# A vision transformer layer on one core: small products behind the gate projection, a softplus behind the next decay, and a reordered start

## The reference

```python
h = layernorm(tokens @ W) * gamma
x = layernorm(h)                                # 16 heads of 64, 256 tokens
q, k = silu(x @ Wq), silu(x @ Wk); v = x @ Wv
log_alpha = -softplus(x @ Wa + ba)              # one per token and head
cum = cumsum(log_alpha, over tokens)
attn = (q @ k.T) * exp(cum_i - cum_j)           # for j <= i, else 0
o = attn @ v                                    # per head
o = (o - mean) / sqrt(var + eps) * gn_w + gn_b  # mean, var over tokens and one head
h = h + (o * sigmoid(x @ Wg)) @ Wo
# the top 2 of 8 experts per token, softmax weights, gelu
h = h + sum_e w_e * (gelu(layernorm(h) @ w1[e] + b1[e]) @ w2[e] + b2[e])
```

## Time and profile before

| | us |
|---|---|
| median of 3 runs | 1318.67 |
| lowest, highest | 1316.14, 1321.25 |
| the profiled execution | 1316.64 |
| its span | 1314.6 |
| PE busy | 1251.5 (95%) |
| PEld busy | 1072.4 (82%) |
| DVE busy | 824.6 (63%) |
| ACT busy | 858.2 (65%) |
| POOL busy | 425.4 (32%) |

### The profile page before, as it was taken

How to read it: one execution, slowest core, us unless ns; L and a number is a source line. 1 busy time by engine, 2 the same in 40 slices (tenths; PEclk the granted TensorE clock), 3 DMA queues, 4 the chain that set the end, 5 groups by cost and what they waited for, 6 DMA issues and landing times. The chain is left out here.

```text
span 1314.6 us, 27299 instructions
## 1 busy us (share of the span) xinstructions
PE 1251.5 (95%) x8534; PEld 1072.4 (82%) x8534; DVE 824.6 (63%) x2120; ACT 858.2 (65%) x2019; POOL 425.4 (32%) x524
## 2 busy tenths in 40 slices
PE   6799999999999999999999999999999999999996
PEld 4576877877877877878878768889899999989996
DVE  4456466566666566665665566657788888555562
ACT  3567567667567567576576465637788888666662
POOL 2111211241241241241241132154445544434433
PEclk8899999999999999999999899999999999999998
DMA  5423222242231341341331335468987886888883
GB/s 185 143 100 90 78 91 88 77 129 74 93 122 55 110 132 49 116 131 47 114 116 56 101 95 193 151 186 245 278 232 220 230 242 184 250 271 269 251 239 83
DMA packets 125607, 194.46 MB, mean 148 GB/s; under 512 B 16272, under 2 KB 91504, under 8 KB 125360
## 3 DMA queue, kind: packets, MB, share of 16 engines
q1 hardware_dynamic: 110864, 175.37, 41.5%
q0 software_dynamic: 13584, 17.26, 6.4%
q10 hardware_dynamic: 1056, 0.55, 0.2%
HBM read 167.40 MB, written 29.05 MB: 149 GB/s over the span
## 5 line engine op out<-in xcount | busy, mean ns | idle before, releaser
L1190 PE MATMUL bank<-xn_sp,big_r 128*128 128x512 f32 x1152 | 315.2, 411 | 2.2 <-DVE big_r L1694 1.7
L1190 PEld LDWEIGHTS bank<-xn_sp,big_r 128*128 128x128 f32 x1152 | 206.6, 190 | 56.4 <-issue 2.4
L837 ACT ACTIVATE dec_x<-dec_x,ncum 128x256 f32<-128x256 f32 (+1 forms) x512 | 189.7, 444 | 10.4 <-POOL dec_x L663 10.4
L1717 DVE TENSOR_TENSOR att<-bank,dec_x 128x384 f32<-128x384 f32 x256 | 130.6, 552 | 102.7 <-PE bank L1229 100.8
L663 POOL TENSOR_SCALAR_AFFINE_SELECT dec_x<-dec_x 128x256 f32<-128x256 f32 x256 | 101.7, 427 | 225.2 <-DMA dec_x<-cum_scratch 224.9
L1535 PE MATMUL bank<-big_r 128*128 128x256 f32 x1296 | 168.0, 286 | 1.9 <-ACT mid_f L907 1.3
L1535 PEld LDWEIGHTS bank<-big_r 128*128 128x128 f32 x1296 | 160.5, 192 | 3.6 <-ACT mid_f L907 1.7
L714 POOL TENSOR_SCALAR mid_f<-mid_f,dec_x 128x256 f32<-128x256 f32 x71 | 77.5, 1096 | 184.7 <-DVE mid_f L1968 182.3
L720 POOL DMA_INDIRECT out<-mid_f,tok x71 | 117.8, 1660 | 53.7 <-POOL mid_f L714 20.2
L1984 DVE TENSOR_TENSOR big_r<-mid_f,big_r 128x256 fp32r<-128x256 f32 x216 | 91.2, 423 | 69.5 <-ACT big_r L927 69.5
L907 ACT ACTIVATE mid_f<-bank,h 128x256 f32<-128x256 f32 x216 | 101.3, 478 | 43.9 <-PE bank L1535 21.6
(11 more groups left out here) (231 smaller groups left out, 2224.5 us busy)
## 6 DMA issues: line engine op xcount, KB each, us to landing
big_f<-in_L_ffn_w SPq DMA_DIRECT2D x68, 1024.0 KB, 6.4
dec_x<-cum_scratch SPq DMA_DIRECT2D x128, 384.0 KB, 3.5
big_w<-in_L_ffn_w SPq DMA_DIRECT2D x12, 1024.0 KB, 6.4
mid_f<-expert_rows SPq DMA_DIRECT2D x27, 261.0 KB, 3.2
h<-h_scratch SPq DMA_DIRECT2D x8, 512.0 KB, 4.6
out<-h SPq DMA_DIRECT2D x16, 256.0 KB, 4.0
xt<-in_x SPq DMA_DIRECT2D x15, 256.0 KB, 3.8
h_scratch<-h SPq DMA_DIRECT2D x15, 256.0 KB, 2.6
```

The lines of the kernel that those rows point to most:

```text
L837: act.activation(d, d, ACT.Exp, bias=ncum[p % 2][:, NS * u + s, 2 * c + hh:2 * c + hh + 1]).then_inc(M["exp_done"], 1)
L1190: mm = pe.matmul(bank[target][:, :], wp[:, k, c * P:(c + 1) * P], xp[:, k, :], start=(k == 0 and j == 0), stop=(k == EC - 1 and j == 2))
L1717: dve.tensor_tensor(att[hh][:, :], bank[4 + hh][:, 0:LW], dec[n % RING][:, hh, :], ALU.mult).then_inc(M["mult_done"], 1)
```

## The change

- **Order within a step, PE.** `gn_var` (steps 0 and 5), `turn(2p+2)` (step 1) and `logits(p+1)` (step 4) move from between `keys` and `gates` to behind `gates`, ahead of the second weighted sum; `logits` goes behind `out_proj`.
- **ACT.** In `last_step`, `keep_o(p, 6)` comes first instead of behind `xn_hi` and the first `y_hi`. `softplus(p+1)` in step 5 moves from ahead of `tanh_k` to behind the second `decay`. `keep_xnT` and `scaled_h` of step 1 move behind `tanh_g`.
- **DVE.** `decay_logits` moves from the end of step 4 to the head of step 5; in step 0 `embed` comes ahead of `affine`, in step 5 `log_decay` ahead of `affine`.
- **The start.** SP waits for the token weights, the four constants and image 1 before it issues the first weight loads. ACT splits weight 3 ahead of softplus, and `scaled_h(0)`, `scaled_h(1)` go behind `tanh_g(0, 0)`; both decays come last. PE runs `cum(0)` ahead of the values and `cum_rows(0)` behind the first. DVE moves `weight_lo(2)` behind `silu_q`.
- **Tiles.** Image 1's h and normalised tokens lie in `h2` and `xn2` instead of in the buffer of the values, so `keep_v` no longer waits for the stores of h.

```diff
         eps0 = sb("eps0", [P, NS])
         pick = sb("pick", [P, TP, TOPK, X])
+        h2 = sb("h2", [P, TP, E])
+        xn2 = sb("xn2", [P, TP, EW])
...
-        side_h = [h1, mid_f[:, 2816:3328].rearrange("p (s n) -> p s n", s=NS)]
-        side_n = [xn1, mid_f[:, 3328:3840].rearrange("p (s n) -> p s n", s=NS)]
+        side_h = [h1, h2[:, 0:NS, :]]
+        side_n = [xn1, xn2[:, 0:NS, 0:E]]
...
             load_patches(0)
             load_patches(1)
+            sp.wait_ge(M["wt_in"], 32)
+            sp.wait_ge(M["c_in"], 64)
+            sp.wait_ge(M["xt_in1"], 32)
             load_weight(0)
             load_weight(1)
             load_patches(2)
...
                 if p == 0 and t >= NS and n == 0:
                     act.wait_ge(M["tok_ps"], 2)
-                    act.wait_ge(M["h_out"], 32)
...
             def last_step(p):
                 main, nxt = pair(p), pair(p + 1)
+                if main:
+                    keep_o(p, 6)
                 if nxt:
                     xn_hi(p + 1)
                 if main:
                     y_hi(p, 0, 0)
-                    keep_o(p, 6)
...
-                if c == 5 and nxt:
-                    softplus(p + 1)
                 if c == 6 and main:
                     affined(p, 0, 0)
                 if main:
@@ -982,12 +983,11 @@
                     decay(p, c + 1, 1)
                     if c in (1, 2):
                         keep_v(p, c + 4, 0)
+                if c == 5 and nxt:
+                    softplus(p + 1)
...
-                if c == 1 and nxt:
-                    keep_xnT(2 * p + 2)
-                    scaled_h(2 * p + 2)
...
                 if main:
                     tanh_g(p, c + 1)
+                if c == 1 and nxt:
+                    keep_xnT(2 * p + 2)
+                    scaled_h(2 * p + 2)
...
             xn_hi(0)
+            weight_hi(3)
             softplus(0)
+            tanh_q(0, 0)
+            keep_v(0, 0, 2)
+            keep_cum(0)
+            for i in range(1, TP):
+                keep_v(0, i, 2 + i)
+            tanh_k(0, 0)
+            tanh_g(0, 0)
             scaled_h(0)
             scaled_h(1)
-            tanh_q(0, 0)
-            keep_cum(0)
-            weight_hi(3)
-            for i in range(TP):
-                keep_v(0, i, 2 + i)
             decay(0, 0, 0)
-            tanh_k(0, 0)
-            tanh_g(0, 0)
             decay(0, 0, 1)
...
-                if c == 0 and post:
-                    gn_var(p - 1, 1)
-                if c == 1 and nxt:
-                    turn(2 * p + 2)
...
-                if c == 4 and nxt:
-                    logits(p + 1)
-                if c == 5 and main:
-                    gn_var(p, 0)
...
                 if main:
                     gates(p, c + 1)
+                if c == 0 and post:
+                    gn_var(p - 1, 1)
+                if c == 5 and main:
+                    gn_var(p, 0)
+                if c == 1 and nxt:
+                    turn(2 * p + 2)
                 if c == 3 and nxt:
                     turn(2 * p + 3)
                 if c == 4 and post:
                     out_proj(p - 1, 1, 1, 7, "h2_done", 2 * p - 1)
+                if c == 4 and nxt:
+                    logits(p + 1)
...
             queries(0, 0)
+            cum(0)
             values(0, 0, 2, "s1_xnT", 2)
+            cum_rows(0)
             values(0, 1, 3, "s1_xnT", 2)
-            cum(0)
             values(0, 2, 4, "s1_xnT", 2)
-            cum_rows(0)
...
+                if c == 5 and nxt:
+                    decay_logits(p + 1)
                 if c == 5 and post:
                     residual(2 * p - 1)
...
                 if c == 0:
+                    if nxt:
+                        embed(2 * p + 2)
                     if post:
                         affine(2 * p - 1)
-                    if nxt:
-                        embed(2 * p + 2)
...
-                if c == 4 and nxt:
-                    decay_logits(p + 1)
                 if c == 5:
+                    if nxt:
+                        log_decay(p + 1)
                     if main:
                         affine(2 * p)
-                    if nxt:
-                        log_decay(p + 1)
...
-            weight_lo(2)
             running_sums(0)
             silu_q(0, 0)
+            weight_lo(2)
             weight_lo(3)
```

More of the change, by code:

```diff
@@ L166, in vit_layer @@
         xs = sb("xs", [P, EC, SP2])
-        h2 = sb("h2", [P, TP, E])
-        xn2 = sb("xn2", [P, TP, EW])
         cumT = sb("cumT", [TP * H, P])
```

## The result

The changed kernel takes 1332.91 us (median of 4 runs, 1331.56 to 1336.52); the kernel before, beside it, 1319.58 (1316.14 to 1321.25). The ratio is 1.0109, with an interval of 1.008 to 1.0138: about 14 us slower. The profiled execution took 1332.95 us with a span of 1330.9, so 16.3 more span than before. I had forecast 1324.0. The time is 9 us above that. It lies in my whole range (1311 to 1334), but not in the forecast's own (1317 to 1331); the whole range went that high for a late gate at the start (rival C), which did not come, so it is luck that it holds the time.

A forecast was written before the change was run, and what follows sets the result against it. TensorE was taken as the bound; -7.5 + 8.95 + 2.0 + 1.0 + 0.9 = +5.35 on 1316.64 gave 1322.0, plus 2.03 to the median 1324.0 us. Forecast's own range 1317 to 1331, whole range 1311 to 1334.

The forecast's parts named there:

- rival C: Start: wa_sb still lands near 14 us, so the weights start 6 us later; +6 us, 1330, chance 0.11.
- step 7, copy first: Step 7: keep_o(p,6) first on ScalarE shortens PE's waits and keeps its clock up; -7.5 us, bounds -6 to -9.
- softplus late, pairs 1 to 6, full clock: Step 6: scores wait goes, but route and decayed(6,0) come later; +1.0 us net in each of pairs 1 to 6.
- the clock behind it: Step 6, pairs 1 to 6: no clock fall behind the new 1.4 us gap counted in the sum.
- log_decay ahead of affine, pair 0: Step 6 of pair 0: +0.95 us delay, plus 2.0 for low clock after about 2.45 us of PE idle.
- embed ahead of affine: Steps 0 and 1: pair 1's weighted sum ends about 1.2 us later, later pairs 0.15 each; +2.0, bounds +1 to +5.
- small products: Turn, logits and variance products beside the second weighted sum may lose overlap; +1.0 us, bounds 0 to 3.
- start: Start: first weighted sum at 51.5 after about 11 us of PE idle, then low clock; +0.9 us, bounds -1 to +3.5.
- rival B: Step 6 of every pair: clock falls behind the new gap, six times 2.0 us more; 1336, chance 0.10.
- the second chain: Step 6: log_decay waits for Ln ahead of affine, delaying GpSimd's rsqrt and decayed(6,0) from 312.83 to 313.86.
- A: Step 6: softplus has room, the old waits vanish with nothing in return; -4.2 instead of +8.95, 1310.8, chance 0.16.
- D: Softplus on ScalarE: table loads hold it longer than their rows, 2.76 us in six pairs; +16.6, 1340.6, chance 0.02.

The follow-up runs named there:

- e3: The kernel before with keep_o(p, 6) first in last_step on ScalarE and nothing else; 1310.98 us, ratio 0.9932.
- e13: The kernel before with softplus(p+1) in step 5 moved behind the second decay and nothing else; 1336.03 us, ratio 1.0143.
- e6: The changed kernel with affine ahead of log_decay again in step 5 on VectorE; 1331.47 us, ratio 1.0091.
- e7: The changed kernel with affine ahead of embed again in step 0; 1330.00 us, ratio 1.0081.
- e4: The kernel before with only gn_var, turn and logits behind gates and decay_logits at the head of step 5; 1318.35 us, ratio 1.0009.
- e8: The kernel before with the change's whole new start alone, including the tiles of image 1; 1318.98 us, ratio 1.0001.
- e5: The changed kernel with keep_x2(2p-2) ahead of keep_o(p,5) in step 6 on ScalarE; 1328.83 us, ratio 1.0076.
- e2: The changed kernel with store_cum(0) and the four decay loads ahead of the two h stores on SP; 1325.17 us, ratio 1.0045.
- e11: The changed kernel with softplus behind tanh_k but ahead of decay(6,1), and keep_x2 ahead of keep_o in step 6; 1311.39 us, ratio 0.9961.
- e1: The changed kernel with softplus(p+1) back ahead of tanh_k in step 5; 1315.79 us, ratio 0.9974.
- e12: The changed kernel with softplus back ahead of tanh_k, store_cum(0) and decay loads before the h stores, embed behind affine; 1299.09 us, ratio 0.9862.
- e14: The changed kernel with softplus ahead of decay(6,1), keep_x2 before keep_o, store_cum(0) and decay loads before h stores, embed behind affine; 1298.31 us, ratio 0.9838.

## Why the prediction was right in part, and where it failed

| term | predicted | measured, and by what |
|---|---|---|
| step 7, copy first | -7.5 | -9.0 (e3, 0.0068 x 1318; interval -11.7 to -6.2); -7.1 in its trace |
| softplus late, pairs 1 to 6, full clock | +6.0 (1.0 each) | 1.23 each (e13, pair 1) |
| the clock behind it | 0 | +1.5 or 3.1 in 4 to 6 pairs of 6 |
| softplus late in all | +6.0 | +18.8 (e13, 0.0143 x 1318; 14.5 to 23.1) |
| log_decay ahead of affine, pair 0 | +2.95 | +3.16 (trace of e6) |
| embed ahead of affine | +2.0 | 1.42 in the stretch of pair 0, 0.37 in each later one (trace of e7) |
| small products | +1.0 | pairs 0.32 shorter each; in all +1.2 (e4, -1.3 to +3.6) |
| start | +0.9 | +0.1 (e8, -2.2 to +2.6) |

*Step 7* was right in its mechanism, its idle time (1.3) and its clock. In pair 7 0.61 us are left for the 0.6 forecast, though on att and no longer on the copy.

*Steps 5 and 6.* The step that failed is "route, which PE would reach at 312.27, starts at 313.66", 1.4 us of idle, with the clock's fall behind it put at nothing in the sum. I had followed x2_done to route alone. `cum` stands ahead of route on PE and waits for the same copy, because it writes bank 6, from which keep_x2 of the even image reads. So the two products of `cum`, the 0.46 us from 319.50 to 319.96, which I had counted as run during the wait, come after it: the idle time is 1.72 and not 1.4. In length this is small (1.23 for 1.0 a pair). But 1.72 was past the 1.55 up to which I had seen the clock hold, and that was my own rival B: six falls at 2.0 each, 1336. It came true in pairs 2 to 6 of the changed kernel. From their stretches, less the 101.16 of the pair that kept its clock: 3.12 and three times 1.54, 7.7 us in pairs 2 to 5, and pair 6 on top. That is most of the 9 us by which the forecast is short.

Rival B's condition was wrong too, though. I had given a threshold between 1.55 and 1.95 us of idle, from two single places. e5 has 1.23 and falls in five pairs of six. Had I known, B would have been the forecast with 1.4 as well. Two rows behind other stretches of work were taken for a rule.

*Pair 0* came as worked out: the second chain only, 2.68 us of idle for 2.45, low clock behind it (0.76 from 117.90 to 124.90). With the same idle e2 kept its clock there, so the 2.0 put down for it came in one kernel and not in the other.

*Rivals A, C and D.* A (room for softplus) is refuted for the place the change takes, though e11 shows that with softplus 1.48 us sooner and the copy of x2 put first there is room indeed. C (late gate) too: PE's first queries start at 26.86, against 28.95 before. For D the step from Abs to tanh_g is 3.42 us with two loads in it, in pair 2 after as before, and in e11 (309.54 to 312.95) as well, 3.41: no hold of ScalarE beyond the loads' own 1.28. The Trainium skill ("ScalarE: Activation LUTs", What ACT_TABLE_LOAD costs) adds 1.38 of drain to each switch; the traces here don't show it.

*Embed first.* The wait on att was 0.93 for a forecast 0.8. In later pairs I had 0.15 and the stretches say 0.37; no wait of PE in the trace explains the difference, and it stays open.

*The start.* The order of events came as written (first store after 40, first weighted sum 52.28 for 51.5, 10.55 us of idle), and e2 shows the cause. I undersized the restart (2.0; by e2 against the changed kernel 2.3) and took one execution's start for the kernel's.

*The sum of the parts.* By the times of one-part kernels: -9.0 (e3) + 18.8 (e13) + 1.2 (e4) + 0.1 (e8), then 2.4 (e6) and 3.7 (e7) from the changed kernel's side, 17.2, against 14.4 measured. Each has an interval of 2 to 4 us to either side, so they agree. A full-clock pair closes more sharply: 100.36 + 1.23 - 0.46 - 0.32 + 0.37 = 101.18, and the changed kernel's pair 1 took 101.16.

## What to carry to other kernels

Before a producer is moved later, list every instruction of the consumer's queue that waits for it, not only the one whose data it makes: here a product that shared a bank stood in front and turned 1.4 us of idle into 1.72. Price a new recurring idle stretch with and without a clock fall, and do not put the fall at nothing because a few single places kept the clock; here it came in 30 of the 36 pairs with a gap of 1.23 to 1.72 us. Softplus 1.5 us sooner, with the copy of x2 put first, was worth 1.5% of the kernel (from 1.0109 to 0.9961), about half of it the clock: in pairs 1 to 5 7.7 of 15.9 us. A store that someone far away waits for goes ahead in its queue of stores that nobody waits for.

## What the runs showed of the hardware

The fall of TensorE's clock doesn't follow from the length of the idle time alone. Ahead of `cum` or the scores of step 6, pairs 1 to 6:

| idle, us | kernels | pairs of six with a fall |
|---|---|---|
| 1.72 | after, e2, e6, e7 | 5, 6, 5, 4 |
| 1.66 | e13 | 5 |
| 1.23 | e5 | 5 |
| 0.53 to 0.61 | before, e1, e3, e4, e8, e12 | 0 |
| none seen | e11, e14 | 0 |

Pairs with the same instructions and the same idle time come out either way. Other places show the same:

- ahead of step 7 of pair 6, 1.31 (e3, 724.56), 1.32 (after, 743.88) and even 1.70 (e11, 723.36) and 1.74 (e14, 708.71) left the clock at 2.4 GHz; 3.20 to 3.22 (before, e4, e8, e13) never did;
- in pair 0, 2.68 let it fall in after, e5 and e7 and left it in e2;
- in pair 7, 1.95 to 2.06 let it fall in 13 of the 14 kernels and left it in e12.

So 1.23 us before `cum` was followed by a fall in five pairs of six where 1.74 elsewhere was not. What PE did before these places differs, and no run here says what of it counts. At step 6 a fall cost 1.4 to 1.6 us or 3.1, with nothing between.
